# A gather stage in which VectorE forms the weighted one-hot rows that GpSimd formed, and three blocks of work stand later in a half batch

## The chip, the core and the metric

The kernel runs on one core of a Trainium2 chip. The metric is device time in microseconds for one whole execution. A core has TensorE (PE in the profile; PEld is its weight load), VectorE (DVE), ScalarE (ACT), GpSimd (POOL) and SyncE (SP, which issues the transfers here). Each engine runs its own instruction stream in order; streams meet only at semaphores.

## What is computed

Two blocks in a row. The first is chunked attention with a residual and a normalisation over time, for 32 batches of 128 channels and 1024 points. The second finds for each of the 1024 points its 30 nearest points, turns the relative coordinates into attention weights, and adds the weighted sum of the neighbours' channels. The part that the change touches is the last:

```
xk = x.transpose(0, 2, 1)[bidx, idx]            # 30 neighbours of each point, all 128 channels
agg = jnp.einsum('bnkc,bnk->bnc', xk, att)      # weighted by the attention
return x + agg.transpose(0, 2, 1)
```

`idx` comes from the nearest-neighbour search, `att` from a small network with a softmax; both are ready when the stage begins.

## The kernel before

Earlier stages (attention, neighbour search, the small network) take the first 5671 us. They stand in other functions and neither the change nor the prediction touches them. The last stage, `stage_e`, does the gather without any indexed read: it multiplies one-hot matrices.

A batch of 1024 points is worked in two half batches of 512 points; n = 2b + q numbers the 64 half batches (q is 0 or 1). The index of a neighbour is cut into a low digit (0 to 127) and a high digit (0 to 7). For each half batch:

- `turn_pairs` (TensorE, L1660, five transposes) turns the digits and the attention, which is split in three bf16 parts, so that the 120 partitions are 30 neighbours by 4 points. ScalarE copies them out of PSUM (`pairs`, L1485).
- `heat` (VectorE, L1603) writes `hot`, the one-hot row of the high digit.
- `weigh` (GpSimd, L1560) writes `wgt`, three products of `hot` with one part of the attention each.
- `spread` multiplies each `wgt` part by four masks into `spr` (`planes` in the profile). Part 0 is done by ScalarE (four instructions, L1491), parts 1 and 2 by VectorE (four each, L1611).
- VectorE writes the one-hot rows of the low digit, `oh`, in eight pieces g = 0 to 7 (L1636), into a ring of four buffers.
- `attend(g)` (TensorE, L1681) multiplies piece g with the three `spr` parts in 48 matmuls into one of two PSUM buffers, `a_ps[g % 2]`. ScalarE's `moved(g)` (L1500) copies it to `at`. `attend(g)` waits until `moved(g - 2)` is done, since it writes the same buffer.
- `gathered` (TensorE, L1694, 16 matmul records in fp32) multiplies `at` with the transposed `x` into `o_ps`. It is run one half batch late: `gathered(n - 1)` stands behind `attend(1)` of half batch n, since it needs all eight `moved` of n - 1. VectorE's `add` (L1620) adds `x`, and SyncE stores.
- Once per batch: `normalise` (L1473) and the copy `turned_rows` (L1480) on ScalarE, `turn_rows` (L1669) on TensorE, `cut` on VectorE, `norm` and `rows` on GpSimd (L1531 to L1549).

What is prepared for half batch n + 1 (pairs, hot, wgt, spr) is prepared while n is worked. `spr` and `pairs` have two buffers, `hot` and `wgt` one. The order on each engine is written out by hand in its `emit`. Before, ScalarE's order in a half batch is pairs, moved(0), moved(1), spread of part 0 for n + 1, moved(2) to moved(7). VectorE's is oh(0 to 2), heat, oh(3), oh(4), spread part 1, oh(5), spread part 2, add, oh(6), oh(7). TensorE's is turn_pairs(n + 1), attend(0), attend(1), gathered(n - 1), in odd half batches turn_rows, attend(2) to attend(7). Batches 2 to 29 run in a loop of 14 turns, two batches (four half batches) a turn.

Of the kernel before, what the change touches and what calls it, by code (L numbers as in the profile page):

```python
# [1351 lines left out]
def stage_e(nc, con, planes, idx_all, stats_all, y_dram, out):  # L1352
# [5 lines left out]
    with ExitStack() as st:  # L1358
# [60 lines left out]
        def passed(value):  # L1419

            return not isinstance(value, int) or value > 0
# [39 lines left out]
        @block.scalar  # L1461
        def _(act):
            a = nc.scalar
            act.wait_ge(ln_step, 1)
            a.activation(rstd[:], stats_all[:, :, 1], ACT.Sqrt, bias=epsc[:]).then_inc(sd_ready, 1)

            def normalise(b, j, par):
                act.wait_ge(y_landed[par], (j + 1) * 16)
                act.wait_ge(norm_ready, b + 1)

                if passed(b - 1):
                    act.wait_ge(o_added, (b - 1) * QUADS)
                a.activation(x1[:, par, :], y_s[:, par, :], ACT.Identity, scale=nrm[:, 0:1], bias=nrm[:, 1:2]).then_inc(x1_ready, 1)  # L1473

            def turned_rows(b, par):
                act.wait_ge(x1_turned, b + 1)

                if passed(b - 1):
                    act.wait_ge(o_ready, (b - 1) * QUADS)
                a.copy(xT[:, par].rearrange("p t c -> p (t c)"), tr_ps[:].rearrange("p a b -> p (a b)")).then_inc(xT_ready, 1)  # L1480

            def pairs(n, q):

                act.wait_ge(pairs_turned, n + 1)
                a.copy(pairs_s[pp, q], pairs_ps[pp]).then_inc(pairs_ready, 1)  # L1485

            def spread(n, q):

                act.wait_ge(weighted, n * PARTS + 1)
                for t in range(QT):  # L1490
                    m = a.activation(spr[q][pp, 0, t], wgt[pp, 0], ACT.Copy, scale=con["tmask"][pp, t:t + 1])  # L1491
                m.then_inc(spread_first, 1)

            def moved(n, q, g):
                act.wait_ge(a_ready, n * NGR + g + 1)

                if g == 0 and passed(n - 1):
                    act.wait_ge(o_ready, n - 1)
                dst = at[:, q, :, :, bass.ts(g, NB)].rearrange("p e t n -> p n t e")
                a.copy(dst, a_ps[g % 2][:]).then_inc(a_moved, 1)  # L1500

            def emit(b, j, par, last):
                for q in range(QUADS):
                    n = b * QUADS + q
                    ahead = not (last and q == QUADS - 1)
                    if ahead:
                        pairs(n + 1, 1 - q)
                    if q == QUADS - 1 and not last:
                        normalise(b + 1, j if par == 0 else j + 1, 1 - par)
                    for g in range(NGR):  # L1510
                        moved(n, q, g)
                        if g == 1 and ahead:
                            spread(n + 1, 1 - q)
                        if g == 3 and q == QUADS - 1 and not last:
                            turned_rows(b + 1, 1 - par)

            normalise(0, 0, 0)
            pairs(0, 0)
            turned_rows(0, 0)
            spread(0, 0)  # L1520
            batches(act, emit)

        @block.gpsimd
        def _(pool):
            v = nc.gpsimd

            def norm(b):

                if passed(b):
                    gate(pool, x1_ready, b, e_pool_gates)  # L1530
                v.tensor_copy(nrm[:, 0:1], rstd[:, bass.ds(b, 1)])  # L1531
                v.tensor_copy(nrm[:, 1:2], nmr[:, bass.ds(b, 1)]).then_inc(norm_ready, 1)

            def rows(b):

                whole = planes[:, 0, bass.ds(b * BCOLS, BCOLS)]
                n = b * (PARTS - 1) + b

                if passed(b):
                    gate(pool, pairs_turned, b * QUADS, e_pool_gates)  # L1540
                v.tensor_copy(rowsb[:, DIGITS, :], whole).then_inc(part_step, 1)
                gate(pool, part_step, n + 1, e_pool_gates)
                v.tensor_tensor(rest[:], whole, rowsb[:, DIGITS, :], ALU.subtract).then_inc(part_step, 1)
                gate(pool, part_step, n + 2, e_pool_gates)
                v.tensor_copy(rowsb[:, DIGITS + 1, :], rest[:]).then_inc(part_step, 1)
                pool.wait_ge(part_step, n + 3)
                v.tensor_tensor(rowsb[:, DIGITS + 2, :], rest[:], rowsb[:, DIGITS + 1, :], ALU.subtract).then_inc(rows_ready, 1)
                gate(pool, digits_cut, (b + 1) * DIGITS, e_pool_gates)
                v.tensor_copy(rowsb[:, 0:DIGITS, :], dig16[:]).then_inc(rows_ready, 1)  # L1549

            def weigh(n, q):

                pool.wait_ge(hot_ready, n + 1)

                if passed(n):
                    pool.wait_ge(spread_first, n)
                    pool.wait_ge(spread_last, n * (PARTS - 1))
                for part in range(PARTS):
                    att = pairs_s[pp, q, DIGITS + part, :].rearrange("p (n o d) -> p n o d", o=1, d=2)
                    v.tensor_tensor(wgt[pp, part], hot[pp], att.to_broadcast([QCOLS, P // 2, HI, 2]), ALU.mult).then_inc(weighted, 1)  # L1560

            def emit(b, j, par, last):
                for q in range(QUADS):
                    if not (last and q == QUADS - 1):
                        weigh(b * QUADS + q + 1, 1 - q)
                    if q == 0 and not last:
                        norm(b + 1)
                        rows(b + 1)

            pool.wait_ge(ln_step, 5)  # L1570
            norm(0)
            rows(0)
            weigh(0, 0)
            batches(pool, emit)

        @block.vector
        def _(dve):
# [18 lines left out]
            def heat(n, q):  # L1596

                dve.wait_ge(pairs_ready, n + 1)

                if passed(n):  # L1600
                    dve.wait_ge(weighted, n * PARTS)
                high = pairs_s[pp, q, 1, :].rearrange("p (n o d) -> p n o d", o=1, d=2)
                v.tensor_tensor(hot[pp], high.to_broadcast([QCOLS, P // 2, HI, 2]),  # L1603
                                hiio[pp].rearrange("p (o e) d -> p o e d", o=1).to_broadcast([QCOLS, P // 2, HI, 2]),
                                ALU.is_equal).then_inc(hot_ready, 1)

            def spread(n, q, part):

                dve.wait_ge(weighted, n * PARTS + part + 1)
                for t in range(QT):  # L1610
                    m = v.tensor_scalar(spr[q][pp, part, t], wgt[pp, part], con["tmask"][pp, t:t + 1], None, ALU.mult)  # L1611
                m.then_inc(spread_last, 1)

            def add(n, b, q, par):

# [6 lines left out]
            def emit(b, j, par, last):  # L1622
                for q in range(QUADS):
                    n = b * QUADS + q
                    if q == 0 and not last:
                        cut(b + 1)

                    dve.wait_ge(pairs_ready, n + 1)
                    for g in range(NGR):
                        gg = n * NGR + g  # L1630

                        if passed(gg - RING + 1):
                            dve.wait_ge(a_ready, gg - RING + 1)
                        low = pairs_s[pp, q, 0, bass.ts(g, NB)].rearrange("p (n o d) -> p n o d", o=1, d=2)
                        row = iotan[pp].rearrange("p (o l) d -> p o l d", o=1)
                        v.tensor_tensor(oh[pp, g % RING], low.to_broadcast([QCOLS, NB // 2, LO, 2]),  # L1636
                                        row.to_broadcast([QCOLS, NB // 2, LO, 2]), ALU.is_equal).then_inc(oh_ready, 1)
                        if g in (4, 5) and not (last and q == QUADS - 1):
                            spread(n + 1, 1 - q, g - 3)
                        if g == 5 and passed(n):  # L1640
                            add(n - 1, b if q == 1 else b - 1, 1 - q, par if q == 1 else 1 - par)
                        if g == 2 and not (last and q == QUADS - 1):
                            heat(n + 1, 1 - q)

            cut(0)
            heat(0, 0)
            for part in range(1, PARTS):
                spread(0, 0, part)
            batches(dve, emit)
            add(B * QUADS - 1, B - 1, 1, 1)  # L1650

# [90 lines left out]
```

## Time and profile before

| | us |
|---|---|
| median of 3 runs | 7002.95 (7002.74 to 7014.98) |
| the profiled execution | 7007.53 |
| its span, first to last instruction | 7005.7 |
| last stage, from 5671 us to the end | 1335 |
| a half batch in it, mean | 20.9 |

Over the whole span VectorE is busy 80%, TensorE 71%, ScalarE 57% and GpSimd 40%. These shares mix stages with different limits, so the last stage has to be read by itself: by its groups of instructions, by a table of stretches with the busy time of each engine, and by the order in time of a few half batches. In those rows a start is given in us from the beginning of the span, then the time the group took; `x4` counts instructions; a bracket gives the idle time of the engine ahead of them and what ended it.

### The profile page before, as it was taken

How to read it: one execution, taken by the hardware profiler on the slowest of the kernel's cores; microseconds unless marked ns; L12 is line 12 of the kernel's file. 1: busy time of each engine (PE TensorE's matmuls, PEld its weight loads, DVE VectorE, ACT ScalarE, POOL GpSimd, SP SyncE). 2: the span in 40 equal slices, each digit the busy share in tenths (PEclk: the TensorE clock that was granted, in tenths of full speed). 3: DMA queues.
4: the chain of work that ended last, by engine and by line, in shares of the span. 5: the costliest groups of instructions: out<-in, count | busy, mean ns of one | idle time of the engine just before them, and what ended most of it. 6: DMA issues, size and time to landing. Idle time of an engine off the chain costs nothing. (4 is left out here: it accounts for less than half of the span.)

```text
span 7005.7 us, 167053 instructions
## 1 busy us (share of the span) xinstructions
PE 4995.6 (71%) x63824; PEld 2914.5 (42%) x63824; DVE 5607.1 (80%) x6966; ACT 4002.8 (57%) x8974; POOL 2816.6 (40%) x3300
## 2 busy tenths in 40 slices
PE   6887878878878787788877878872000058888888
PEld 3444444444444444444444444441000046666666
DVE  8877877877778777787877778764789888888887
ACT  4666655666666656565655656564222256666666
POOL 2444444544445444444444454441000034444443
PEclk8788878788878877888788788775555579998989
DMA  1000000000000000000000000000000000000000
GB/s 37 13 14 14 14 23 16 13 14 14 14 26 14 14 13 14 25 14 14 13 14 14 25 14 14 13 10 1 0 0 0 0 20 27 31 27 28 27 27 27
DMA packets 35795, 114.00 MB, mean 16 GB/s; under 512 B 5488, under 2 KB 6128, under 8 KB 34800
## 3 DMA queue, kind: packets, MB, share of 16 engines
q1 hardware_dynamic: 34928, 102.28, 4.1%
q8 instruction: 564, 9.24, 0.6%
q14 instruction: 303, 2.48, 0.1%
HBM read 68.71 MB, written 33.55 MB: 15 GB/s over the span
## 5 line engine op out<-in xcount | busy, mean ns | idle before, releaser
L550 ACT ACTIVATE ohT<-oh_ps,cst 128x512 bf16<-128x512 f32 x1920 | 1277.4, 691 | 389.1 <-PE oh_ps L430 384.0
L448 PE MATMUL g_ps<-tparts,ohT 128*128 128x24 bf16 x23040 | 921.7, 178 | 795.9 <-ACT ohT L550 785.5
L448 PEld LDWEIGHTS g_ps<-tparts,ohT 128*128 128x128 bf16 x23040 | 765.7, 100 | 1439.3 <-ACT ohT L550 1335.8
L794 DVE MAX8 vals<-pd_sb 128x8 f32<-128x1024 f32 x1024 | 1205.3, 1213 | 134.2 <-ACT pd_sb L550 112.5
L799 DVE FIND_INDEX8 idx<-vals,pd_sb 128x8 uint16<-128x1024 f32 x1024 | 1244.2, 1218 | 0.0
L801 DVE MATCH_REPLACE8 pd_sb<-vals,pd_sb 128x1024 f32<-128x1024 f32 x768 | 927.8, 1208 | 0.0
L430 PE MATMUL oh_ps<-bitsT,code 128*128 128x512 bf16 x1920 | 875.2, 461 | 2.2 <-ACT bitsT L707 2.2
L550 ACT ACTIVATE pd_sb<-pd_ps,nxx 128x512 f32<-128x512 f32 x512 | 355.1, 694 | 863.9 <-PE pd_ps L354 862.5
L818 DVE TENSOR_REDUCE mx<-s_ps 128x8 f32<-128x512 f32 x256 | 176.4, 689 | 722.0 <-PE s_ps L389 722.0
L1560 POOL TENSOR_TENSOR e_wgt<-e_hot,e_pairs 120x1024 bf16<-120x1024 bf16 x192 | 478.4, 2516 | 660.7 <-DVE e_hot L1603 660.7
L1681 PE MATMUL e_a_ps<-planes,e_oh 120*128 120x32 bf16 x24576 | 673.5, 179 | 92.9 <-DVE e_oh L1636 53.9
L1500 ACT COPY e_at<-e_a_ps 128x512 f32<-128x512 f32 x512 | 546.2, 1093 | 302.9 <-PE e_a_ps L1681 287.9
L1681 PEld LDWEIGHTS e_a_ps<-planes,e_oh 120*128 120x128 bf16 x24576 | 658.5, 98 | 125.2 <-DVE e_oh L1636 63.1
L1636 DVE TENSOR_TENSOR e_oh<-e_pairs,e_iotan 120x2048 bf16<-120x2048 bf16 x512 | 700.2, 1411 | 0.5 <-PE e_a_ps L1681 0.5
L352 PE MATMUL pd_ps<-ctx_s 128*128 128x512 f32 x1024 | 657.8, 729 | 0.0
L689 ACT ACTIVATE sS<-s_ps,mx 128x64 f32<-128x64 f32 x2048 | 611.0, 337 | 64.3 <-DVE mx L818 34.3
L860 POOL TENSOR_TENSOR gsb<-gsb,hi1h 128x480 f32<-128x480 f32 x384 | 396.1, 1032 | 591.5 <-ACT gsb L620 591.5
L354 PE MATMUL pd_ps<-sq,neghalf 128*128 128x512 f32 x1024 | 597.6, 669 | 0.0
L863 POOL TENSOR_TENSOR gsb<-gsb 128x240 f32<-128x240 f32 (+2 forms) x1152 | 553.6, 481 | 90.3
L963 POOL CAST bitsb<-bits 128x1024 bf16<-128x1024 uint16 x64 | 118.5, 1851 | 1046.9 <-DVE bits L752 1046.9
L953 POOL TENSOR_TENSOR kz<-kt,cst 128x1024 f32<-128x1024 f32 x256 | 488.0, 1906 | 16.0 <-ACT kt L550 16.0
L1694 PE MATMUL e_o_ps<-e_at,e_xT 128*128 128x512 f32 x1024 | 474.8, 618 | 1.3 <-ACT e_at L1500 1.1
(200 smaller groups left out, 7519.0 us busy)
## 6 DMA issues: line engine op xcount, KB each, us to landing
ctx_s<-in_ctx SPq DMA_DIRECT2D x32, 512.0 KB, 4.3
maskb<-in_mask_Bx1x_ff SPq DMA_DIRECT2D x32, 512.0 KB, 5.1
x_s<-in_x SPq DMA_DIRECT2D x32, 512.0 KB, 5.8
y_spill<-y_s SPq DMA_DIRECT2D x32, 512.0 KB, 2.9
e_y<-y_spill SPq DMA_DIRECT2D x32, 512.0 KB, 3.7
out<-e_o SPq DMA_DIRECT2D x64, 256.0 KB, 2.0
pd_sb<-in_shape_constants SPq DMA_DIRECT2D x1, 1024.0 KB, 5.0
cst<-in_shape_constants SPq DMA_DIRECT2D x1, 242.5 KB, 2.7
```

The source lines that it names most:

```text
L352: nc.tensor.matmul(pd_ps[:, h, :], ctx_s[:, par, bass.ts(t, P)], ctx_s[:, par, bass.ts(h, HALF)], start=True, stop=False)
L354: nc.tensor.matmul(pd_ps[:, h, :], neghalf[:], sq[:, bass.ts(h, HALF)], start=False, stop=True).then_inc(pd_ready, 1)
L430: nc.tensor.matmul(oh_ps[k % 2][:], code[:, k % KT, :], bitsT[:, k // KT, :], start=True, stop=True).then_inc(oh_ready, 1)
L448: m = nc.tensor.matmul(g_ps[:, k % GK, t, :], ohT[:, k % 2, bass.ts(t, P)], tparts[:, par, part, :], start=(part == 0), stop=(part == PART ...
L550: return nc.scalar.activation(dst, src, func, scale=scale, bias=bias)
L689: m = nc.scalar.activation(sS[:, t % 2, hd, :], s_ps[:, hd, :], ACT.Exp, bias=mx[:, t % 2, hd:hd + 1], accum_out=rs[:, t % 2, hd:hd + 1])
L794: nc.vector.max(vals[:, i, :], pd_sb[:, (t + i) % RING, :]).then_inc(topk_step, 1)
L799: found = nc.vector.max_index(idx16[:, par, t + i, 8 * r:8 * r + 8], vals[:, i, :], work)
L801: nc.vector.match_replace(work, vals[:, i, :], work, REMOVED).then_inc(topk_step, 1)
L863: steps(nc.gpsimd.tensor_tensor(sums[:, :, 0:width], sums[:, :, 0:width], sums[:, :, width:2 * width], ALU.add))
L1636: v.tensor_tensor(oh[pp, g % RING], low.to_broadcast([QCOLS, NB // 2, LO, 2]), row.to_broadcast([QCOLS, NB // 2, LO, 2]), ALU.is_equal).th ...
L1681: m = nc.tensor.matmul(a_ps[g % 2][:, i].rearrange("p t e -> p (t e)"), oh[pp, g % RING, i // 2, :, i % 2], spr[q][pp, part, :, (g * NB + ...
```

## The change

VectorE does `weigh`, one part behind each of oh(3), oh(4) and oh(5). Its two spreads move from behind oh(4) and oh(5) to behind oh(6) and oh(7). ScalarE's spread moves from behind moved(1) to behind moved(3), and its `turned_rows` from behind moved(3) to behind moved(5). GpSimd keeps `norm` and `rows`. TensorE's instructions and their order are what they were. `heat` no longer waits for the weighting, since both are on one engine now.

```diff
@@ ScalarE, emit @@
                     for g in range(NGR):
                         moved(n, q, g)
-                        if g == 1 and ahead:
+                        if g == 3 and ahead:
                             spread(n + 1, 1 - q)
-                        if g == 3 and q == QUADS - 1 and not last:
+                        if g == 5 and q == QUADS - 1 and not last:
                             turned_rows(b + 1, 1 - par)
@@ GpSimd @@
-            def weigh(n, q):
-
-                pool.wait_ge(hot_ready, n + 1)
-
-                if passed(n):
-                    pool.wait_ge(spread_first, n)
-                    pool.wait_ge(spread_last, n * (PARTS - 1))
-                for part in range(PARTS):
-                    att = pairs_s[pp, q, DIGITS + part, :].rearrange("p (n o d) -> p n o d", o=1, d=2)
-                    v.tensor_tensor(wgt[pp, part], hot[pp], att.to_broadcast([QCOLS, P // 2, HI, 2]), ALU.mult).then_inc(weighted, 1)
-
             def emit(b, j, par, last):
-                for q in range(QUADS):
-                    if not (last and q == QUADS - 1):
-                        weigh(b * QUADS + q + 1, 1 - q)
-                    if q == 0 and not last:
-                        norm(b + 1)
-                        rows(b + 1)
+                if not last:
+                    norm(b + 1)
+                    rows(b + 1)
@@ VectorE @@
-                if passed(n):
-                    dve.wait_ge(weighted, n * PARTS)
...
+            def weigh(n, q, part):
+
+                if part == 0:
+                    dve.wait_ge(hot_ready, n + 1)
+                    if passed(n):
+                        dve.wait_ge(spread_first, n)
+                elif passed(n):
+                    dve.wait_ge(spread_last, n * (PARTS - 1) - (PARTS - 1) + part)
+                att = pairs_s[pp, q, DIGITS + part, :].rearrange("p (n o d) -> p n o d", o=1, d=2)
+                v.tensor_tensor(wgt[pp, part], hot[pp], att.to_broadcast([QCOLS, P // 2, HI, 2]), ALU.mult).then_inc(weighted, 1)
...
-                        if g in (4, 5) and not (last and q == QUADS - 1):
-                            spread(n + 1, 1 - q, g - 3)
+                        if g in (3, 4, 5) and not (last and q == QUADS - 1):
+                            weigh(n + 1, 1 - q, g - 3)
+                        if g in (6, 7) and not (last and q == QUADS - 1):
+                            spread(n + 1, 1 - q, g - 5, range(QT))
```

How ScalarE's order moves, at the passage from an even half batch (first row: its last copies of `at`) into an odd one, in the part behind the loop, where no register instructions stand between. Before:

```order
1014 L1500 COPY e_at<-e_a_ps 128x16x4x8 x6
1015 L1485 COPY e_pairs<-e_pr_ps 120x640
1016 L1473 ACTIVATE e_x<-e_y,e_nrm 128x1024
1017 L1500 COPY e_at<-e_a_ps 128x16x4x8 x2
1018 L1491 ACTIVATE planes<-e_wgt,cst 120x1024 x4
1019 L1500 COPY e_at<-e_a_ps 128x16x4x8 x2
1020 L1480 COPY e_xT<-e_tr_ps 128x1024
1021 L1500 COPY e_at<-e_a_ps 128x16x4x8 x4
```

And in the changed kernel, the same engine and place:

```order
1014 L1500 COPY e_at<-e_a_ps 128x16x4x8 x4
1015 L1485 COPY e_pairs<-e_pr_ps 120x640
1016 L1473 ACTIVATE e_x<-e_y,e_nrm 128x1024
1017 L1500 COPY e_at<-e_a_ps 128x16x4x8 x4
1018 L1491 ACTIVATE planes<-e_wgt,cst 120x1024 x4
1019 L1500 COPY e_at<-e_a_ps 128x16x4x8 x2
1020 L1480 COPY e_xT<-e_tr_ps 128x1024
1021 L1500 COPY e_at<-e_a_ps 128x16x4x8 x2
```

The four masks of ScalarE's spread stood behind two copies of `at` and stand behind four.

VectorE, one half batch in the same part. Before:

```order
1082 L1603 TENSOR_TENSOR e_hot<-e_pairs,e_hiio 120x1024
1083 L1636 TENSOR_TENSOR e_oh<-e_pairs,e_iotan 120x2048 x2
1084 L1611 TENSOR_SCALAR planes<-e_wgt,cst 120x1024 x4
1085 L1636 TENSOR_TENSOR e_oh<-e_pairs,e_iotan 120x2048
1086 L1611 TENSOR_SCALAR planes<-e_wgt,cst 120x1024 x4
1087 L1620 TENSOR_TENSOR e_o<-e_o_ps,e_x 128x512
```

And in the changed kernel:

```order
1123 L1586 TENSOR_TENSOR e_hot<-e_pairs,e_hiio 120x1024
1124 L1631 TENSOR_TENSOR e_oh<-e_pairs,e_iotan 120x2048
1125 L1599 TENSOR_TENSOR e_wgt<-e_hot,e_pairs 120x1024
1126 L1631 TENSOR_TENSOR e_oh<-e_pairs,e_iotan 120x2048
1127 L1599 TENSOR_TENSOR e_wgt<-e_hot,e_pairs 120x1024
1128 L1631 TENSOR_TENSOR e_oh<-e_pairs,e_iotan 120x2048
1129 L1599 TENSOR_TENSOR e_wgt<-e_hot,e_pairs 120x1024
1130 L1615 TENSOR_TENSOR e_o<-e_o_ps,e_x 128x512
1131 L1631 TENSOR_TENSOR e_oh<-e_pairs,e_iotan 120x2048
1132 L1605 TENSOR_SCALAR planes<-e_wgt,cst 120x1024 x4
1133 L1631 TENSOR_TENSOR e_oh<-e_pairs,e_iotan 120x2048
1134 L1605 TENSOR_SCALAR planes<-e_wgt,cst 120x1024 x4
```

Three weightings have come into VectorE's stream, and both blocks of four spreads have moved past the add (`e_o`), to the end.

## Rows read from the trace of the kernel before

**Rows 1.** Table of stretches: the stage, then four half batches of one loop turn.

```profile
core 0: us, PE busy (x) PEld busy (x) DVE busy (x) ACT busy (x) POOL busy (x), PEclk, DMA share, GB/s
5671.00:7006.00 1335.00, 1179.84 (x26158) 903.22 (x26158) 1128.05 (x1213) 907.86 (x892) 624.64 (x408) 0.90 0.08 27
...
6342.27:6362.06 19.79, 18.75 (x412) 13.75 (x409) 17.97 (x19) 13.89 (x15) 12.03 (x11) 0.93 0.05 16
6362.06:6381.95 19.89, 18.73 (x421) 14.60 (x417) 17.93 (x22) 14.60 (x15) 8.09 (x4) 0.91 0.13 43
6381.95:6401.47 19.52, 17.70 (x412) 13.61 (x408) 17.68 (x18) 13.81 (x15) 11.65 (x11) 0.91 0.05 16
6401.47:6425.42 23.95, 18.70 (x419) 14.57 (x416) 17.71 (x21) 14.82 (x15) 7.87 (x4) 0.89 0.12 36
```

**Rows 2.** Groups of the last stage: form and count, busy us, mean ns, idle before.

```profile
L1636 DVE TENSOR_TENSOR e_oh<-e_pairs,e_iotan 120x2048 bf16<-120x2048 bf16 x512 | 700.2, 1411 | 0.5 <-PE e_a_ps L1681 0.5
...
L1560 POOL TENSOR_TENSOR e_wgt<-e_hot,e_pairs 120x1024 bf16<-120x1024 bf16 x191 | 476.5, 2519 | 657.7 <-DVE e_hot L1603 657.7
...
L1611 DVE TENSOR_SCALAR planes<-e_wgt,cst 120x1024 bf16<-120x1024 bf16 x512 | 361.0, 764 | 128.1 <-POOL e_wgt L1560 128.1
...
L1603 DVE TENSOR_TENSOR e_hot<-e_pairs,e_hiio 120x1024 bf16<-120x1024 bf16 x63 | 43.4, 690 | 61.0 <-ACT e_pairs L1485 60.1
```

**Rows 3.** TensorE in order of time, 6340 to 6440 us.

```profile
6342.27 8.47 PE L1694 MATMUL e_o_ps<-e_at,e_xT 128*128 128x512 f32 x16
...
6375.60 2.71 PE L1681 MATMUL e_a_ps<-planes,e_oh 120*128 120x32 bf16 x96 [0.47 <-ACT e_at L1500]
...
6380.20 1.90 PE L1681 MATMUL e_a_ps<-planes,e_oh 120*128 120x32 bf16 x69 [0.59 <-issue]
...
6388.90 5.23 PE L1681 MATMUL e_a_ps<-planes,e_oh 120*128 120x32 bf16 x192
6395.86 2.72 PE L1681 MATMUL e_a_ps<-planes,e_oh 120*128 120x32 bf16 x96 [1.73 <-DVE e_oh L1636]
...
6401.47 7.11 PE L1694 MATMUL e_o_ps<-e_at,e_xT 128*128 128x512 f32 x16
6408.42 1.04 PE L1669 MATMUL e_tr_ps<-cst,e_x 128*128 128x128 f32 x8
6409.29 5.23 PE L1681 MATMUL e_a_ps<-planes,e_oh 120*128 120x32 bf16 x192
...
6422.24 0.78 PE L1660 MATMUL e_pr_ps<-e_identb,e_rowsb 128*120 128x128 bf16 x5 [4.70 <-issue]
```

**Rows 4.** ScalarE in order of time, 6350 to 6440 us.

```profile
6374.36 2.02 ACT L1500 COPY e_at<-e_a_ps 128x512 f32<-128x512 f32 x2
...
6390.30 2.33 ACT L1500 COPY e_at<-e_a_ps 128x512 f32<-128x512 f32 x2 [2.27 <-PE e_a_ps L1681]
...
6404.01 4.26 ACT L1491 ACTIVATE planes<-e_wgt,cst 120x1024 bf16<-120x1024 bf16 x4 [0.81 <-POOL e_wgt L1560]
```

**Rows 5.** VectorE in order of time, 6350 to 6440 us.

```profile
6394.59 5.75 DVE L1636 TENSOR_TENSOR e_oh<-e_pairs,e_iotan 120x2048 bf16<-120x2048 bf16 x5
...
6406.88 3.33 DVE L1611 TENSOR_SCALAR planes<-e_wgt,cst 120x1024 bf16<-120x1024 bf16 x4 [1.82 <-POOL e_wgt L1560]
...
6411.26 1.66 DVE L1611 TENSOR_SCALAR planes<-e_wgt,cst 120x1024 bf16<-120x1024 bf16 x4
```

**Rows 6.** Durations of the one-hot rows, shortest, median and longest in ns.

```profile
L1636 DVE TENSOR_TENSOR e_oh<-e_pairs,e_iotan x512: 1204/1211/2957, 5676.2 to 6987.4; 120x2048 bf16<-120x2048 bf16 x171
```

**Rows 7.** Waits of the last stage: us in total, times, longest.

```profile
PE e_pr_ps L1660 <- issue: 61.0, 15, 5.0
```

**Rows 8.** Stretches of 6395 to 6427 us; PEclk is the granted TensorE clock.

```profile
6395.86:6401.47 5.61, 5.61 (x198) 5.61 (x198) 5.59 (x6) 3.95 (x5) 0.25 (x1) 0.70 0.12 42
...
6422.24:6425.42 3.18, 3.18 (x101) 3.18 (x102) 1.54 (x2) 1.70 (x2) 0.61 (x1) 0.50 0.02 5
6425.42:6427.00 1.58, 1.58 (x9) 0.82 (x5) 1.58 (x2) 1.15 (x2) 1.58 (x1) 0.52 0.04 10
```

More of the change, by code:

```diff
@@ L1572, in _ @@
             rows(0)
-            weigh(0, 0)
             batches(pool, emit)
@@ L1605, in heat, with spread @@
                                 ALU.is_equal).then_inc(hot_ready, 1)
-            def spread(n, q, part):
+            def weigh(n, q, part):
[7 more added lines that the diff above has]
+                v.tensor_tensor(wgt[pp, part], hot[pp], att.to_broadcast([QCOLS, P // 2, HI, 2]), ALU.mult).then_inc(weighted, 1)
+            def spread(n, q, part, rows):
                 dve.wait_ge(weighted, n * PARTS + part + 1)
-                for t in range(QT):
+                for t in rows:
                     m = v.tensor_scalar(spr[q][pp, part, t], wgt[pp, part], con["tmask"][pp, t:t + 1], None, ALU.mult)
-                m.then_inc(spread_last, 1)
+                if rows[-1] == QT - 1:
+                    m.then_inc(spread_last, 1)
             def add(n, b, q, par):
@@ L1646, in _ @@
             heat(0, 0)
+            for part in range(PARTS):
+                weigh(0, 0, part)
             for part in range(1, PARTS):
-                spread(0, 0, part)
+                spread(0, 0, part, range(QT))
             batches(dve, emit)
```

## The prediction

> **What bounds the kernel now.** Read the table of stretches first [rows 1]. The last stage takes 1335 us and holds 64 half batches. The four below it are one loop turn, each from the start of one `gathered` to the start of the next: 19.79, 19.89, 19.52 and 23.95 us, together 83.15. TensorE is busy 17.7 to 18.8 us in each, VectorE 17.7 to 18.0, ScalarE 13.8 to 14.8. So TensorE is nearest to full; the fourth stretch holds a pause of 4.70 us that TensorE makes at the loop's branch [rows 3], one of 15 in the stage with 61.0 us in all [rows 7].
>
> What TensorE cannot go below comes from its own rows [rows 3]. `gathered` occupies it for 6.95 us (6401.47 to 6408.42), `turn_rows` for 0.87 (to 6409.29, odd half batches only), four `attend` for 5.0 to 5.1 (5.23 shown, the last result's latency in it), and from the start of attend(6) to the next `gathered` 5.61 pass (6395.86 to 6401.47: attend(6), attend(7), turn_pairs, attend(0), attend(1)). That is 6.95 + 5.1 + 5.6 = 17.65 us in an even half batch and 18.5 in an odd one. The difference to 19.5 and more is a wait for VectorE: 1.73 us ahead of attend(6) in the row at 6395.86.
>
> VectorE is late there because of GpSimd. A weighting takes GpSimd 2519 ns [rows 2], and VectorE's first block of spreads waits 1.82 us for it [rows 5]. One-hot rows take 1211 ns in the median and up to 2957 [rows 6]; in the mean 1411 [rows 2], that is 8 x 0.2 = 1.6 us a half batch lost while GpSimd works. So the chain hot, weigh, spread, oh(6) sets most of the periods now.
>
> **What the change removes.** From GpSimd three weightings a half batch, 7.5 us; nobody else on GpSimd waits for that, its `rows` come early either way. From VectorE the wait of 1.82 us and most of the stretching. Added to VectorE are three weightings. No row shows one; the nearest is the row of `hot`, same shape, same types, two inputs from SBUF, 690 ns [rows 2], so 3 x 0.69 = 2.1 us. As bounds I keep 0.45 us each (a mask costs VectorE 1.66 / 4 [rows 5], from one input) and 2.5 us each (GpSimd's time), and take 0.69. The waits in front of them end long before: the mask blocks of the half batch before are through by then.
>
> Does VectorE hold TensorE up afterwards? Count from the end of `gathered`, t = 0, even half batch. attend(2) is through at 1.40 (ScalarE's copy of it starts at 6390.30 where attend(2) began at 6388.90 [rows 3, 4]). oh(6) may then run, 1.14 (five in 5.75 [rows 5]), mask block 1.6, oh(7) 1.14, mask block 1.6: done at 6.9. With GpSimd's `rows` beside both blocks each would take about 2.9 or 3.3 instead, as a block does at 6406.88 [rows 5]: then 10. TensorE needs the masks only for the next attend(0), at 12 or later (below). Before `gathered` VectorE has from attend(7) on three oh, `hot` and three weightings, 3 x 1.14 + 4 x 0.69 = 6.2 us, beside 3.1 us of TensorE (turn_pairs to attend(1)) and 6.95 of `gathered`. So the weightings cost nothing while this cover of 10 us stands; at 2.5 us each they would be 11.6 and push the add by 2 to 4 us, still hidden in the 5 us between 6.9 and 12.
>
> **What it moves.** This is the part that decides. ScalarE's four masks stood behind moved(1), in the shadow of `gathered`, when ScalarE has nothing else to do. Behind moved(3) they cannot start before TensorE has done attend(3), which comes after `gathered`. And attend(6) waits for moved(4), which now stands behind them. From t = 0:
> - moved(2) starts at 1.40, moved(3) 1.25 later at 2.65; the two take 2.33 in all and end at 3.73 [rows 4].
> - The four masks take 4.26 to 4.27 [rows 4], ScalarE overlapping neighbours by about 0.1 (two copies in 2.02 [rows 4], where one takes 2.33 - 1.25 = 1.08): 3.63 to 7.9.
> - moved(4) runs 7.8 to 8.9.
> - attend(6) starts 0.15 later (copy done at 6375.45, attend at 6375.60 [rows 3, 4]): t = 9.0.
> - TensorE was through with attend(5) at 5.1, so it stands 3.9 us.
>
> From attend(6) to the next `gathered` 5.6 us pass as before: moved(5), moved(6) and moved(7) follow each other at 1.0 to 1.25 us and keep up with attends of 1.25. In odd half batches `turned_rows` behind moved(5) adds 1.0; moved(6) is then through at about attend(6) + 3.1, and attend(0) wants it at attend(6) + 3.1: nothing, or 0.1. The period is 6.95 + 9.0 + 5.6 = 21.55 us in an even half batch, and 22.4 with `turn_rows`.
>
> **The sum.** One loop turn: 2 x 21.55 + 2 x 22.4 = 87.9. The branch pause stays, 4.7. Behind it the clock is low (0.50, and 0.52 in the first 1.58 us of `gathered` [rows 8]), so that `gathered` takes 8.47 instead of 7.11 in one such turn, 1.4 lost at worst [rows 3], and by the 1.58 us at half clock 0.8 in the other; between nothing and 1.4 I take 0.7. Now this is hidden, since VectorE is the late one; then it shows: 0.7. Together 93.3 against 83.15, which is 10.15 a turn or 2.54 a half batch. 62 half batches have a `gathered` and a spread for a next one: 157 us. Another pause of TensorE, 0.59 at 6380.20 [rows 3], once a turn, lies in VectorE's lateness now; it may show or be taken up by the new stall, 0 to 8 us over 14 turns, I take 5. So +162 on the profiled execution, 7007.5 + 162 = 7169.5. That execution is 4.6 us over the median of the runs, so 7165 on the scale of the median.
>
> **The clock.** The row says: behind a pause of 1.73 us TensorE's mean clock is 0.70 over the 5.61 us of attends [rows 8], that is, part of it at 1.2 GHz, and the following `gathered` still runs in its 7.11 us, at 2.4 GHz [rows 3]. The attends scarcely feel it: turn_pairs and two attends take 3.18 us at clock 0.50 [rows 8], and 0.6 + 2.5 at the full clock. With a stall of 3.9 us ahead of the same 5.6 us of attends I take `gathered` to start at the full clock. The Trainium skill has a rule against this change: "TensorE: Matmul & The Clock Gate", section "HAM oscillation — how this bites in real kernels", says that idle gaps between bursts of matmuls throw the engine back to half its clock and the next burst pays. Read so that each `gathered` starts slow, it gives the second case below; the row at 6401.47 speaks against it, the one at 6342.27 for it.
>
> **The rivals.**
> 1. The forecast: the stall on moved(4), 7165. Chance 0.84.
> 2. The same stall, and each `gathered` behind it starts at half clock. 1.4 to 1.7 us for each, as at 6342.27 at worst, x 62 = 87 to 105 us: 7260. For it: a stall of 3.9 us is closer to the branch pause of 4.7 than to the 1.73 that did no harm. Against it: 5.6 us of matmuls stand between, not 3.2. Chance 0.08.
> 3. VectorE becomes the bound. Its work is 9.1 (oh) + 0.6 (hot) + 2.1 + 3.3 + 0.7 (add) + 0.15 = 16 us, below 21.5. It takes weightings of 2.5 us together with blocks of 3.3 to reach 25, which would give about 7300. Chance 0.02.
> 4. Faster. The masks are in effect hidden and the freed VectorE leaves TensorE at its own 17.65 and 18.5: 72.3 + 4.7 + 0.7 = 77.7 a turn, 5.45 less, x 15.5 = 84 us, 6918. This decides for itself at the point where ScalarE's work between moved(3) and moved(4) fits under attend(4) and attend(5): 5.1 - 0.15 - 1.1 = 3.85 is when moved(4) would have to start, so about 0.3 us of masks, where four take 4.2. It would come about if the order of the streams did not bind as I read it. "GPSIMD Engine Reference" of the Trainium skill, section "4.1 Engine selection", would lead one to expect this side: it sends two-input elementwise work to VectorE as about twice as fast, and the trace bears that out (2519 against 690 ns for this shape). Chance 0.04.
> 5. Gain and stall cancel: the stall would have to be 1.4 us instead of 3.9, masks of about 0.4 us each on ScalarE. Its own row says 1.04. Chance 0.02.
>
> **How the numbers follow.** The predicted time is case 1. Its own bounds: a stall of 3.5 to 4.3 us (25 us either way), 0 to 8 for the small pause, 0 to 1.4 for the slow `gathered` behind a branch, and some of case 2 in some half batches, 0.5 us in half of them, 15 us: 7130 to 7215. To leave out no more than 2 in 10 I take 7125 to 7235, toward case 2 more than toward the others. A difference under 0.2% (14 us) cannot be told from none here. Slower: cases 1, 2 and 3, 0.94; same: 0.02; faster: 0.04.
>
> **What would show it.** In the changed kernel's profile: TensorE's waits led by attend for ScalarE's copy of `at`, some 60 of 3 to 4 us, about 240 in all; ScalarE's copies waiting for attends 6 to 8 us during `gathered`; GpSimd nearly idle; one-hot rows at 1.21 in the mean, weightings at 0.69; `gathered` starts 21.5 and 22.4 us apart; the stage near 1497. I am wrong in the step of the masks if the wait ahead of attend(6) is under 3 us, in the clock if `gathered` takes 8 us or more in most half batches, and on VectorE if TensorE waits for `oh` or the masks.

## The result and the profile after

The changed kernel takes 7142.8 us in the median of 4 runs (7122.1 to 7146.6) against 7005.9 (7002.7 to 7015.0) before: ratio 1.0187, 95% interval 1.0165 to 1.021. It is 137 us slower, where 7165 us was forecast, 162 us slower. The profiled execution has a span of 7143.4 us.

The same four half batches as in [rows 1], one loop turn of the changed kernel (columns as there):

```profile
6353.66:6375.15 21.49, 17.80 (x411) 13.74 (x408) 16.90 (x22) 13.38 (x15) 2.48 (x2) 0.84 0.04 14
6375.15:6401.43 26.28, 18.87 (x421) 14.73 (x417) 16.24 (x24) 14.33 (x15) 2.92 (x5) 0.82 0.10 33
6401.43:6423.31 21.88, 18.20 (x411) 13.92 (x408) 16.72 (x22) 13.24 (x15) 3.37 (x3) 0.82 0.04 14
6423.31:6445.68 22.37, 18.69 (x421) 14.56 (x417) 15.74 (x24) 14.30 (x15) 2.77 (x5) 0.92 0.11 38
sum 92.02, PE 73.56 PEld 56.95 DVE 65.60 ACT 55.25 POOL 11.55; mean PE 18.39 PEld 14.24 DVE 16.40 ACT 13.81 POOL 2.89
```

They take 21.49, 26.28, 21.88 and 22.37 us, 92.02 in all, for 83.15 before. VectorE's busy time fell from 71.3 to 65.6 in the turn and GpSimd's from 39.7 to 11.6, although VectorE took the weighting over. No engine has more to do than before, and yet the turn is 8.9 us longer. Where TensorE stands idle is told by its own waits, over the stage (us in total, times, longest):

```profile
ACT e_at L1500 <- PE e_a_ps L1680: 523.3, 179, 9.1
...
PE e_a_ps L1680 <- ACT e_at L1500: 225.3, 63, 3.6
...
DVE e_o L1615 <- PE e_o_ps L1693: 156.2, 64, 15.8
...
PE e_pr_ps L1659 <- issue: 51.5, 15, 4.2
```

The row of the kernel before that answers to the second one:

```profile
PE e_a_ps L1681 <- ACT e_at L1500: 20.0, 30, 6.7
```

The wait of attend for ScalarE's copies grew from 20.0 to 225.3 us in 63 waits, one in each half batch that prepares a next one. In order of time, one even half batch on TensorE and the passage at the loop's branch:

```profile
6360.61 5.23 PE L1680 MATMUL e_a_ps<-planes,e_oh 120*128 120x32 bf16 x192
6369.44 2.72 PE L1680 MATMUL e_a_ps<-planes,e_oh 120*128 120x32 bf16 x96 [3.60 <-ACT e_at L1500]
...
6375.15 7.11 PE L1693 MATMUL e_o_ps<-e_at,e_xT 128*128 128x512 f32 x16
...
6398.24 0.78 PE L1659 MATMUL e_pr_ps<-e_identb,e_rowsb 128*120 128x128 bf16 x5 [3.73 <-issue]
...
6401.43 7.54 PE L1693 MATMUL e_o_ps<-e_at,e_xT 128*128 128x512 f32 x16
```

and on ScalarE:

```profile
6362.01 2.33 ACT L1500 COPY e_at<-e_a_ps 128x512 f32<-128x512 f32 x2 [7.10 <-PE e_a_ps L1680]
6364.11 4.25 ACT L1491 ACTIVATE planes<-e_wgt,cst 120x1024 bf16<-120x1024 bf16 x4
6368.27 1.93 ACT L1500 COPY e_at<-e_a_ps 128x512 f32<-128x512 f32 x2
```

`gathered` ends at 6360.61; ScalarE copies moved(2) and moved(3) from 6362.01, then come the four masks, 4.25 us, then moved(4) from 6368.27; attend(6) starts at 6369.44, having waited 3.60 us. The reader can lay this beside [rows 3, 4]: there ScalarE had its masks at 6404.01, under `gathered`. The groups that answer to [rows 2]:

```profile
L1631 DVE TENSOR_TENSOR e_oh<-e_pairs,e_iotan 120x2048 bf16<-120x2048 bf16 x512 | 640.1, 1261 | 118.6 <-PE e_a_ps L1680 118.5
...
L1605 DVE TENSOR_SCALAR planes<-e_wgt,cst 120x1024 bf16<-120x1024 bf16 x504 | 210.5, 481 | 0.0
...
L1599 DVE TENSOR_TENSOR e_wgt<-e_hot,e_pairs 120x1024 bf16<-120x1024 bf16 x189 | 143.9, 761 | 0.0
```

One-hot rows fell from 1411 to 1261 ns, masks from 764 to 481, and the weighting costs VectorE 761 ns, overlap with its neighbour included. All of that was a gain, and none of it reached the end but for some 8 us in the first half batch (below).

### The profile page after: what moved, and what is told of

Same layout as the page of the kernel before. It is cut to its first block and busy times, and to the rows that moved or that the text cites. A ratio compares the mean times of both kernels' runs of the same rounds, so it can differ in the third digit from the quotient of the medians.

```text
span 7143.4 us, 166934 instructions
## 1 busy us (share of the span) xinstructions
PE 4995.5 (70%) x63824; PEld 2920.8 (41%) x63824; DVE 5528.1 (77%) x7158; ACT 3981.5 (56%) x8974; POOL 2379.4 (33%) x3108
## 5 line engine op out<-in xcount | busy, mean ns | idle before, releaser
L1680 PE MATMUL e_a_ps<-planes,e_oh 120*128 120x32 bf16 x24576 | 680.0, 181 | 240.5 <-ACT e_at L1500 225.3
L1631 DVE TENSOR_TENSOR e_oh<-e_pairs,e_iotan 120x2048 bf16<-120x2048 bf16 x512 | 640.1, 1261 | 118.6 <-PE e_a_ps L1680 118.5
L1531 POOL COPY e_nrm<-e_rstd 128x1 f32 (+1 forms) x32 | 21.6, 675 | 1433.9 <-DVE e_nmr L1571 876.9
L953 POOL TENSOR_TENSOR kz<-kt,cst 128x1024 f32<-128x1024 f32 x256 | 488.2, 1907 | 15.5 <-ACT kt L550 15.5
L689 ACT ACTIVATION_READ_ACCUMULATOR sS<-s_ps,mx 128x1 f32 x2048 | 474.6, 232 | 0.0
L1693 PE MATMUL e_o_ps<-e_at,e_xT 128*128 128x512 f32 x1024 | 468.9, 611 | 1.1 <-ACT e_at L1500 1.1
```

The source lines that it names most:

```text
L689: m = nc.scalar.activation(sS[:, t % 2, hd, :], s_ps[:, hd, :], ACT.Exp, bias=mx[:, t % 2, hd:hd + 1], accum_out=rs[:, t % 2, hd:hd + 1])
L1680: m = nc.tensor.matmul(a_ps[g % 2][:, i].rearrange("p t e -> p (t e)"), oh[pp, g % RING, i // 2, :, i % 2], spr[q][pp, part, :, (g * NB + ...
L1693: m = nc.tensor.matmul(o_ps[q][:], xT[:, par, e, :], at[:, q, e].rearrange("p t n -> p (t n)"), start=(e == 0), stop=(e == HI - 1))
```

## The experiments

**What is disputed.** Theory M: the four masks on ScalarE, moved out of the shadow of `gathered`, make attend(6) wait, and that is the whole loss. Theory V: the work added to VectorE, and its mask blocks at the end of a half batch, are what costs. Theory C: the clock behind the new stall.

**Masks put back.** The changed kernel with

```diff
-                        if g == 3 and ahead:
+                        if g == 1 and ahead:
                             spread(n + 1, 1 - q)
-                        if g == 5 and q == QUADS - 1 and not last:
+                        if g == 3 and q == QUADS - 1 and not last:
                             turned_rows(b + 1, 1 - par)
```

> The changed kernel with one thing put back: ScalarE's four masks stand behind moved(1) again and turned_rows behind moved(3). VectorE still does the weighting, its spreads stay behind oh(6) and oh(7). Theory (the masks, moved out of the shadow of gathered, make attend(6) wait for moved(4), 3.6 us in each of 63 half batches): the waits of attend for ScalarE's copies fall from 225 us to under 15, gathered starts stand 17.7 and 18.5 us apart, and the time falls by about 63 x 3.6 = 227 us to 6900 to 6930, below both kernels. Rival (the added work on VectorE, with the spreads at the end of a half batch, is what costs): nothing of that is taken away here, so the time stays at 7100 to 7145, and TensorE waits for VectorE in place of ScalarE.

Measured: 6933.0 us (6927.7 to 6938.8), ratio to before 0.9893 (0.9876 to 0.9909): 210 us under the changed kernel and 1.1% faster than the kernel before. TensorE's waits in this kernel, from 5670 us on:

```profile
PE e_pr_ps L1659 <- issue: 60.1, 17, 4.7
PE e_a_ps L1680 <- ACT e_at L1500: 18.8, 32, 4.4
PE e_a_ps L1680 <- issue: 8.5, 29, 0.5
...
PE e_a_ps L1680 <- DVE e_oh L1631: 0.4, 1, 0.4
```

TensorE waits 0.4 us for one-hot rows and 18.8 us for copies. (The wait of 7.6 us for a one-hot row ahead of the stage's first attend stands in both kernels; here it lies just before 5670 us.) ScalarE now has its masks at 6338.60, 4.26 us, under the `gathered` that starts at 6337.36. Two lines of ScalarE's order decide over 210 us; V falls, since VectorE's work is all there. The even half batches are at TensorE's own 17.6 us, as worked out in the fourth rival of the prediction:

```profile
6337.36 7.11 PE L1693 MATMUL e_o_ps<-e_at,e_xT 128*128 128x512 f32 x16
6344.31 7.89 PE L1680 MATMUL e_a_ps<-planes,e_oh 120*128 120x32 bf16 x288
6352.05 0.47 PE L1659 MATMUL e_pr_ps<-e_identb,e_rowsb 128*120 128x128 bf16 x5
6352.51 2.58 PE L1680 MATMUL e_a_ps<-planes,e_oh 120*128 120x32 bf16 x96
6354.93 7.11 PE L1693 MATMUL e_o_ps<-e_at,e_xT 128*128 128x512 f32 x16
```

From one `gathered` (6337.36) to the next (6354.93) no row carries an idle time. The time missed the expected range by 3 us on the high side.

**Masks late, and nothing else.** The kernel before with the same two edits the other way round (masks at `g == 3`, `turned_rows` at `g == 5`); GpSimd weighs, VectorE's order is the old one.

> The kernel before with one thing changed: ScalarE's four masks behind moved(3) and turned_rows behind moved(5). GpSimd still does the weighting, VectorE's order is the old one. Theory of the masks: the stall of 3.6 us ahead of attend(6) is there as in the changed kernel, GpSimd's slowness lies under it, and the time is 7135 to 7165 (the changed kernel's, plus the 8 us that its first half batch saves). Rival (VectorE's added work costs): VectorE has none of it here, the time is that of before, 6995 to 7020.

Measured: 7149.4 us (7145.7 to 7154.7), ratio 1.0205 (1.0188 to 1.0222). This edit alone makes the loss, and 6.6 us more than the whole change does. From the first `gathered` to the last the two profiled executions take the same, 1440.5 us here and 1441.5 in the changed kernel; what is left is the first half batch, 37.4 us to the first `gathered` here and 29.3 there. GpSimd's weighting disappears under the stall. Behind the first half batch the profile puts 17 of these 62 waits down to VectorE's one-hot row, but they are as long as the others. In the one ahead of 6369.40, 3.58 us, the row is written from 6367.04 in about 1.2 us and ScalarE's copy starts only at 6368.24, so the copy is the later one. With GpSimd weighing, VectorE is about 1 us ahead of it.

**A dose of it.** The changed kernel with masks 0 and 1 behind moved(1), 2 and 3 behind moved(3); `spread` on ScalarE takes the masks that it is to do (that part of the edit is left out here).

```diff
-                        if g == 3 and ahead:
-                            spread(n + 1, 1 - q)
+                        if g == 1 and ahead:
+                            spread(n + 1, 1 - q, (0, 1))
+                        if g == 3 and ahead:
+                            spread(n + 1, 1 - q, (2, 3))
```

> The changed kernel with two of ScalarE's four masks behind moved(1) and two behind moved(3); turned_rows behind moved(5) as in the changed kernel. Two masks take 2 x 1.04 = 2.1 us. Theory of the masks, in numbers: the stall ahead of attend(6) is 3.6 - 2.1 = 1.5 us, the time is lower by 63 x 2.1 = 131 us, 7005 to 7020. If it is not their length but the fact that ScalarE has turned to other work (a threshold, a clock that falls behind any stall), the time stays above 7080.

Measured: 7016.8 us (7007.8 to 7029.9), ratio 1.0013 (1.0003 to 1.0023); 126 us less than four late masks, for 131 expected. The wait behind it:

```profile
PE e_a_ps L1683 <- ACT e_at L1501: 96.9, 64, 2.4
```

64 waits of 1.5 us, where four masks gave 3.6: two masks of 1.04 apart, as the theory says. With no late mask (the first experiment) it is 84 us less again, not 131: the stall cannot go below nothing. Only 96.9 us of it were left, 18.8 of them stay, and TensorE's pauses for which the profile shows no releaser, in its attends and at `turn_pairs`, come to 68.6 us for 56.3.

**Another late place.** The changed kernel with the masks at `g == 5`.

> The changed kernel with ScalarE's four masks behind moved(5) in place of moved(3). Now moved(6) is late, and the next attend(0) waits for it in place of attend(6). Theory (any place outside the shadow of gathered costs about the same, since TensorE gets only two attends ahead of ScalarE): worked out with the same durations, 20.95 us in an even half batch for 21.5 and 22.8 in an odd one for 22.4, where turned_rows comes behind the masks; 7120 to 7150. Rival (the later place gives TensorE time to run ahead and takes the stall away): under 7080.

Measured: 7142.2 us (7140.0 to 7145.4), ratio 1.0191 (1.0174 to 1.0208). The time is as expected, but it is made up otherwise than it was worked out:

```profile
6350.35 0.47 PE L1659 MATMUL e_pr_ps<-e_identb,e_rowsb 128*120 128x128 bf16 x5
6354.44 2.74 PE L1680 MATMUL e_a_ps<-planes,e_oh 120*128 120x32 bf16 x96 [3.63 <-ACT e_at L1500]
6357.02 8.49 PE L1693 MATMUL e_o_ps<-e_at,e_xT 128*128 128x512 f32 x16
...
6377.47 2.74 PE L1680 MATMUL e_a_ps<-planes,e_oh 120*128 120x32 bf16 x96 [2.75 <-ACT e_at L1500]
6380.05 8.91 PE L1693 MATMUL e_o_ps<-e_at,e_xT 128*128 128x512 f32 x16
```

The half batch from 6357.02 to 6380.05 takes 23.03 us where 20.95 was worked out, the one before it, with `turn_rows`, 24.17 for 22.8. The stall now stands right ahead of attend(0), 3.6 us in one half batch and 2.8 in the next, so TensorE waits 149 us in all in place of 225. But only two attends, 2.6 us, lie between it and `gathered`. The granted clock is 0.50 through them and 0.53 over the first 2.98 us of `gathered`, that is, still at 1.2 GHz, and 1.00 from there on; `gathered` takes 8.5 and 8.9 us where it takes 7.11 at the full clock. Its records are 663 ns in the mean for 611 in the changed kernel, and it is busy 49 us longer in all (517.9 for 468.9); TensorE's pauses without a releaser come to 73.9 us for 52.1. Together that gives 71 of the 76 us back:

```profile
L1693 PE MATMUL e_o_ps<-e_at,e_xT 128*128 128x512 f32 x1024 | 517.9, 663 | 1.1 <-ACT e_at L1500 1.1
```

So the cost that theory C names is real, and a matter of where the stall stands: in the changed kernel it hardly shows, here it does.

**Only the masks.** The changed kernel with the masks back at `g == 1` and `turned_rows` left at `g == 5`.

> The changed kernel with only ScalarE's four masks put back behind moved(1); turned_rows stays behind moved(5), where the change had put it. In the run with both put back, attend(6) still waits 0.47 us in each odd half batch, since turned_rows (1.0 us) stands between moved(3) and moved(4). Theory: any ScalarE work between moved(3) and moved(4) is paid beyond about 0.4 us, so this wait goes: 31 x 0.47 = 15 us under the 6933 of that run, 6910 to 6925. Rival: attend(0) waits as long for moved(6) instead, and the time stays at 6930 to 6940.

Measured: 6938.9 us (6931.2 to 6954.0), ratio 0.9897 (0.9881 to 0.9914): no gain on 6933.0. The wait for ScalarE goes, 18.8 to 4.6 us, but TensorE's pauses for which the profile shows no releaser grow, from 8.5 to 14.2 inside the attends and from 60.1 to 64.4 at `turn_pairs`:

```profile
PE e_pr_ps L1659 <- issue: 64.4, 18, 4.8
PE e_a_ps L1680 <- issue: 14.2, 38, 0.8
...
PE e_a_ps L1680 <- ACT e_at L1500: 4.6, 2, 4.4
```

The expectation missed; its rival held, though not for the reason it gave: nothing waits for moved(6). In the first odd half batch one can see where the gain goes. With both blocks put back, attend(6) waits 0.46 us for ScalarE and TensorE then pauses 0.35 us behind its first 8 matmuls (at 5700.50); here the wait is gone and the pause at the same matmul (at 5709.78) is 0.62 us. Of the 0.46 us only 0.19 are gained. What the pauses are was not tried. `gathered` is also busy 8.5 us longer in this profiled execution (473.0 for 464.5), which is 15 us over the median of its kernel.

**A longer loop.** On top of that kernel, 7 turns of four batches in place of 14 of two.

```diff
-            with eng.Fori(1, B // 2 - 1) as j:
-                emit(j * 2, j, 0, False)
-                emit(j * 2 + 1, j, 1, False)
+            with eng.Fori(1, B // 4) as j:
+                emit(j * 4 - 2, j * 2 - 1, 0, False)
+                emit(j * 4 - 1, j * 2 - 1, 1, False)
+                emit(j * 4, j * 2, 0, False)
+                emit(j * 4 + 1, j * 2, 1, False)
```

> The kernel of e5 with a loop of 7 turns of four batches in place of 14 turns of two. TensorE stands about 4 us at each branch of the loop (52 us in 15 waits in the changed kernel). Theory (the pause belongs to the branch): 7 of them and the slow start of gathered behind each go, 7 x (4.0 + 0.3) = 30 us, 6880 to 6895. Rival (the pause belongs to fetching new instructions, of which there are as many a batch as before): the time stays within 10 us of e5, the pauses reappear within the longer body.

Measured: 6902.6 us (6893.2 to 6906.6), ratio to before 0.9845 (0.9828 to 0.9861), the fastest of all. It is 36 us under its base, for 30 expected and 8 us above the range. TensorE's pauses ahead of `turn_pairs` fell from 64.4 us in 18 to

```profile
PE e_pr_ps L1661 <- issue: 25.4, 7, 4.5
```

Each of the traces with 14 turns has 13 pauses of 3.5 to 5.0 us ahead of `turn_pairs`, one at the end of each turn but the last; this one, with 7 turns, has 6, of 4.1 to 4.5. The pause belongs to the jump back to the loop's start. Why it is there and what sets its length no run here shows.

**GpSimd weighs, the rest as in the kernel of "only the masks".** This is the kernel before with VectorE's two mask blocks behind oh(6) and oh(7).

```diff
-                        if g in (4, 5) and not (last and q == QUADS - 1):
-                            spread(n + 1, 1 - q, g - 3)
+                        if g in (6, 7) and not (last and q == QUADS - 1):
+                            spread(n + 1, 1 - q, g - 5)
```

(and `turned_rows` at `g == 5`).

> The kernel of e5 with the weighting left on GpSimd, three instructions in a row as before the change; VectorE's two blocks of masks stand behind oh(6) and oh(7), ScalarE's behind moved(1). It differs from e5 in who weighs alone. Theory A (the move of the weighting to VectorE is what gains; GpSimd's weightings hold VectorE's one-hot rows for 2.9 us and its rows stretch the mask blocks to 2.9): in even half batches the second mask block ends at about 9.5 us behind gathered where the next attend(0) wants it at 8.2, so 1.3 us more, and 8 us in the first half batch: 6945 to 6985. Theory B (the gain is from where VectorE's mask blocks stand, behind the wait for gathered, so that GpSimd's slowness is covered whoever weighs): within 15 us of e5 apart from the first half batch, 6915 to 6935. If VectorE were still the late one in every half batch: 6990 to 7010.

Measured: 7005.8 us (6990.8 to 7011.7), ratio 0.9992 (0.9983 to 1.0002): all of the gain is gone. Both theories missed, A by 21 us. The number falls in the third range of the expectation, 6990 to 7010, but not for its reason: VectorE is not the late one in every half batch, since TensorE waits for one-hot rows 28 times, 29.9 us in all. The piece that A names is there: in an even half batch attend(0) waits 0.98 us for VectorE, whose mask blocks are stretched by GpSimd's `rows` to 2.2 and 2.4 us:

```profile
6393.68 2.69 PE L1681 MATMUL e_a_ps<-planes,e_oh 120*128 120x32 bf16 x96 [0.98 <-DVE e_oh L1636]
```

What A lacks is on ScalarE, which now waits 208.2 us for GpSimd's first weighting (56.7 before the change), while VectorE hardly waits for GpSimd any more, 7.6 us for 128.1:

```profile
ACT planes L1491 <- POOL e_wgt L1560: 208.2, 64, 5.2
...
DVE planes L1611 <- POOL e_wgt L1560: 7.6, 2, 3.9
```

GpSimd and VectorE in the same half batch, from `hot` on:

```profile
6358.00 8.81 POOL L1560 TENSOR_TENSOR e_wgt<-e_hot,e_pairs 120x1024 bf16<-120x1024 bf16 x3 [7.57 <-DVE e_hot L1603]
```

```profile
6357.16 0.68 DVE L1603 TENSOR_TENSOR e_hot<-e_pairs,e_hiio 120x1024 bf16<-120x1024 bf16 x1
6357.76 3.48 DVE L1636 TENSOR_TENSOR e_oh<-e_pairs,e_iotan 120x2048 bf16<-120x2048 bf16 x3
```

```profile
6363.06 4.27 ACT L1491 ACTIVATE planes<-e_wgt,cst 120x1024 bf16<-120x1024 bf16 x4 [4.30 <-POOL e_wgt L1560]
```

VectorE runs three one-hot rows without a gap at 1.14 us, unstretched, and this time it is GpSimd that stands: its first weighting takes 5.0 of the 8.81 us, where 2.5 is the mean in [rows 2]. It ends at about 6363.0, 1.8 us after VectorE's third row, and the two weightings behind it, with VectorE idle, take 1.9 us each. ScalarE's masks wait 4.30 us, end at 6367.3, and hold moved(2) and attend(4) back.

TensorE's waits for ScalarE and VectorE in its attends are 36.2 and 29.9 us in this kernel, 4.6 and 8.5 in the other one, and `gathered` is busy 10 us longer behind them: 63 us. Its pauses without a releaser are 13 us shorter, which leaves 50, and from the stage's first transposes to its end this profiled execution is 49 us longer than the other. As a whole it is 45 us longer; the medians are 67 us apart, since the other kernel was profiled in an execution 15 us above its median and this one in an execution 7 us below. So it does matter who weighs, for a reason that neither theory had: the two engines stop each other, and which of them stops changes with the order of VectorE's instructions.

The Trainium skill, "SBUF — State Buffer", section "SBUF: two separate sides", says that VectorE and GpSimd share a pair of ports that one of them holds for a whole instruction while the other is blocked. The trace agrees, with 5.0 us for a first weighting that takes 1.9 when VectorE is idle; it shows in addition that three instructions of VectorE in a row can keep GpSimd out for nearly their whole 3.5 us.

## Why the prediction was right, point by point

- **The step of the masks** held. Forecast: attend(6) at 9.0 us behind `gathered`, a stall of 3.9; measured 8.83 (6360.61 to 6369.44) and 3.60. Even half batches 21.55 against 21.49, odd ones 22.4 against 22.37. The stall is shorter by 0.3. Of this 0.17 is ScalarE, which goes from copies to masks and back a little faster than was added up, 6362.01 to 6368.27 being 6.26 us for the 6.4 in the sum; the other 0.13 is only where attend(5) was taken to end, 5.1 in the sum and 5.23 in the row.
- **VectorE** held: weightings hidden, masks of the next half batch ready at 6367.5, 6.9 us behind `gathered` as counted, needed at 6372.6. TensorE waits 8.6 us for one-hot rows in the stage, 7.6 of them ahead of its first attend.
- **The branch pause** was taken over at 4.7 us and is 3.73 in the turn shown, 51.5 us in 15 waits for 61.0. There are 13 such long pauses in either trace, not one for each of the 15.5 turns of the sum. The slow `gathered` behind one lost 0.57 us in the mean of the 13 (0.4 in the turn shown, 7.54 for 7.11) for 0.7 taken. The small pause counted with 5 us does not show between `turn_pairs` and `gathered`. These terms are too large by 9.5 + (15.5 x 0.7 - 13 x 0.57) + 5, some 18 us together.
- **The first half batch** was left out. There the first weightings have nothing to hide under, 5.7 us on GpSimd before and 2.5 on VectorE now:

```profile
5667.30 5.70 POOL L1560 TENSOR_TENSOR e_wgt<-e_hot,e_pairs 120x1024 bf16<-120x1024 bf16 x3 [3.02 <-DVE e_hot L1603]
5680.40 7.75 POOL L1560 TENSOR_TENSOR e_wgt<-e_hot,e_pairs 120x1024 bf16<-120x1024 bf16 x3 [7.40 <-DVE e_hot L1603]
```

```profile
5663.20 2.52 DVE L1599 TENSOR_TENSOR e_wgt<-e_hot,e_pairs 120x1024 bf16<-120x1024 bf16 x3
```

The first `gathered` starts 37.4 us after the stage's first transposes before (5663.30 to 5700.70) and 29.3 after (5659.24 to 5688.51): 8 us gained. Those transposes themselves stood 4 us earlier in this execution, which is no doing of the change.
- The parts then add up on the two executions: -4.1 before the stage, -8.1 in the first half batch, +148.5 from the first `gathered` to the last (1293.0 to 1441.5), +1.4 behind it: 137.7. The forecast had 162 for the third of these alone. A half batch there grew from 20.52 to 22.88 us in the mean; the forecast had 20.79, from the one turn shown, and 23.3. Both are too large, by 17 and 28 us over its 62 half batches, so that taking the turn shown for a typical one cancelled 17 us of the error. That the time came out within 22 us of the forecast is in part this luck; the length of the stall is not.
- **The clock** held as the row had it: behind the stall the granted clock is 0.51 in the mean, that is 1.2 GHz, through the 5.71 us of attends, and 1.00, 2.4 GHz, when `gathered` starts. The second rival was wrong for this place of the masks. With the masks behind moved(5) it came about: there `gathered` takes 8.09 us in the mean of 64, 1.0 over its 7.11, where the rival took 1.4 to 1.7. The rows of the changed kernel:

```profile
6369.44:6375.15 5.71, 5.71 (x197) 5.71 (x198) 2.88 (x4) 4.82 (x6) 0.00 (x0) 0.51 0.01 3
6375.15:6382.10 6.95, 6.95 (x23) 3.08 (x20) 4.62 (x6) 1.65 (x2) 1.14 (x2) 1.00 0.01 2
```

- **The faster rival** was wrong for this change and right on what it would be worth: with the masks in their old place 6933 was measured for the 6918 worked out there.

## What to carry to other kernels

An engine that is idle a third of the time can still have only one place in its order where its work is free; before a block is moved on it, ask which instruction of the bounding engine waits for what stands behind the block, and add up the chain from there. Moving the weighting from GpSimd to VectorE was worth 1.0% here by the medians (6938.9 against 7005.8), and the same change carried a reordering on ScalarE that cost three times that much: when a change has several parts, time each alone. Here a stall cost by its length and by its distance to the next long matmuls.

## What the runs showed of the hardware that was not expected

- GpSimd can be starved by VectorE. With the masks put back, where VectorE's stream is dense, GpSimd's copy of one element per partition (`e_nrm`, L1531), 0.38 us in the kernel before, takes 5.2 us in the median. In the changed kernel itself, where VectorE has gaps, it takes 0.53. In the kernel of "only the masks" one such copy runs from 6369.00 to 6374.25, and VectorE from 6368.90 on runs three one-hot rows and three weightings without a gap to 6374.1. The row of the masks put back:

```profile
L1531 POOL COPY e_nrm<-e_rstd x29: 4704/5243/5323, 5723.8 to 6833.4; 128x1 f32 x28, 128x1 f32<-128x1 f32 x1
```

Nobody waits for it, so it costs nothing here. Before, the stretching went the other way, one-hot rows up to 2957 ns [rows 6].
- A stall of 3.6 us costs `gathered` nothing more, or 1.4 us more, as 5.7 or 2.6 us of small matmuls lie between the stall and `gathered`. The small matmuls themselves hardly slow down at half the clock: two attends take 2.72 to 2.77 us at 0.50 and 0.51, and 2.58 at 1.00 (6352.51 with the masks put back).
- The pause at the loop's branch is not a constant: 61.0 us in 15 waits before, 51.5 in 15 after, 25.4 in 7 with the longer loop, of which 13, 13 and 6 are the long ones at the jump back. What sets its length stays open.
